# Neighbour sum: preparation two slots earlier, and values transposed by VectorE from 32x32 blocks instead of by TensorE

## The reference, cut to what matters

```python
            att = jax.nn.softmax(h[..., 0], axis=-1)
            xk = x.transpose(0, 2, 1)[bidx, idx]
            agg = jnp.einsum('bnkc,bnk->bnc', xk, att)
            return x + agg.transpose(0, 2, 1)
...
    x = _L2_xattn_ref(ctx_4096, x, L2_xattn_W1, L2_xattn_g1, L2_xattn_b1, L2_xattn_W2, L2_xattn_g2, L2_xattn_b2, L2_xattn_W3, L2_xattn_g3, L2_xattn_b3, 30)
    x = _L3_xattn_ref(x, ctx_4096, ctx_4096, ctx_4096, mask_Bx1x4096_ff1, L3_xattn_W_in, L3_xattn_b_in, L3_xattn_W_out, L3_xattn_b_out)
```

## Time and profile before

| | us |
|---|---|
| median of 3 runs | 6278.45 |
| lowest and highest | 6277.33 and 6285.72 |
| the profiled execution | 6277.67 |
| its span, first to last instruction | 6275.9 |
| TensorE matmuls busy in the span | 5497.9 (88%) |
| VectorE busy | 5659.0 (90%) |
| ScalarE busy | 4493.5 (72%) |
| GpSimd busy | 3395.9 (54%) |

### The profile page before, as it was taken

How to read it: one execution, slowest core, us unless ns; L and a number is a source line. 1 busy time by engine, 2 the same in 40 slices (tenths; PEclk the granted TensorE clock), 3 DMA queues, 4 the chain that set the end, 5 groups by cost and what they waited for, 6 DMA issues and landing times. The chain is left out here.

```text
span 6275.9 us, 227278 instructions
## 1 busy us (share of the span) xinstructions
PE 5497.9 (88%) x82516; PEld 3378.3 (54%) x82516; DVE 5659.0 (90%) x8045; ACT 4493.5 (72%) x17145; POOL 3395.9 (54%) x3471
## 2 busy tenths in 40 slices
PE   7888989889888888888898888898669769999999
PEld 3555555555555555555555555555423347777776
DVE  7999999999999999999999999999755787777776
ACT  7888888888888888888888888888605623333333
POOL 3466666666666666666666666666720033333332
PEclk9999999999999999999999999999789879999999
DMA  2333333333333333333333333333340023333332
GB/s 45 95 105 99 99 99 97 92 99 108 99 111 92 100 98 97 98 106 102 106 98 99 99 98 98 99 108 96 105 99 0 0 70 94 88 85 88 89 93 71
DMA packets 651349, 568.72 MB, mean 91 GB/s; under 512 B 553072, under 2 KB 574832, under 8 KB 616208
## 3 DMA queue, kind: packets, MB, share of 16 engines
q1 hardware_dynamic: 613264, 284.51, 19.3%
q10 hardware_dynamic: 36864, 268.45, 12.2%
HBM read 384.76 MB, written 67.24 MB: 72 GB/s over the span
## 5 line engine op out<-in xcount | busy, mean ns | idle before, releaser
L725 ACT ACTIVATE prob<-SC,row_max 128x64 f32<-128x64 f32 x6144 | 1835.6, 335 | 336.1 <-DVE row_max L1059 327.2
L838 POOL TENSOR_TENSOR prob<-prob,row_rec 128x512 f32<-128x512 f32 x768 | 800.6, 1042 | 1394.3 <-DVE row_rec L1067 1389.4
L725 ACT ACTIVATION_READ_ACCUMULATOR prob<-SC,row_max 128x1 f32 x6144 | 1387.8, 228 | 0.0
L1051 DVE FIND_INDEX8 nbr<-top,dist 128x8 uint16<-128x1024 f32 x1024 | 1234.3, 1217 | 0.0
L1044 DVE MAX8 top<-dist 128x8 f32<-128x1024 f32 x1024 | 1190.6, 1203 | 1.7 <-DVE dist L1046 0.2
L1046 DVE MATCH_REPLACE8 dist<-top,dist 128x1024 f32<-128x1024 f32 x768 | 923.4, 1207 | 0.0
L589 PE MATMUL SC<-k_bd,q_t 128*64 128x256 f32 x6144 | 902.7, 418 | 0.0
L1710 ACT ACTIVATE dense<-DM 128x512 f32<-128x512 f32 x512 | 305.4, 596 | 749.9 <-PE DM L1669 749.4
L1818 DVE TENSOR_TENSOR d_oh_a<-lo,iota_a 128x4096 bf16<-128x4096 bf16 x256 | 583.7, 2290 | 242.2 <-PE DM L1669 241.7
L610 PEld LDWEIGHTS PT<-ident,prob 128*128 128x128 f32 x3072 | 364.0, 144 | 812.3 <-issue 789.1
L610 PE MATMUL PT<-ident,prob 128*128 128x128 f32 x3072 | 487.8, 283 | 334.2 <-ACT prob_t L732 333.5
(11 more groups left out here) (189 smaller groups left out, 9437.9 us busy)
## 6 DMA issues: line engine op xcount, KB each, us to landing
low_all<-low_scratch ACTq DMA_DIRECT2D x256, 1024.0 KB, 5.0
k_bd<-k_t SPq DMA_DIRECT2D x3072, 16.0 KB, 1.9
placed<-compact SPq DMA_DIRECT2D x256, 192.0 KB, 3.8
ctx<-in_ctx SPq DMA_DIRECT2D x32, 512.0 KB, 5.9
mask<-in_mask SPq DMA_DIRECT2D x32, 512.0 KB, 8.5
xb<-in_x SPq DMA_DIRECT2D x32, 512.0 KB, 3.3
x_scratch<-xb SPq DMA_DIRECT2D x32, 512.0 KB, 6.8
y_scratch<-y_b SPq DMA_DIRECT2D x32, 512.0 KB, 6.4
```

What stands on the lines that cost most here:

```text
L725: last = act.activation(prob[:, s % 4, g * CHUNK:(g + 1) * CHUNK], SC[:, s % 2, g * CHUNK:(g + 1) * CHUNK], ACT.Exp, bias=row_max[:, s % 2 ...
L838: pool.tensor_tensor(pr, pr, row_rec[:, r % 2, :].unsqueeze(2).to_broadcast([128, 8, CHUNK]), ALU.mult).then_inc(normed, 1)
L1051: last = dve.max_index(nbr[:, uu % BPB, t, k * 8:(k + 1) * 8], best, row)
```

## The change

TensorE's transposes, `XT`, the identity and ScalarE's copy of `XT` are gone. The values are loaded a second time: ScalarE's queue issues four DMAs per batch (`by_quarters`), each of which fills 32 partitions of `x2_q` with pieces of 32 values (128 bytes), 1024 pieces a DMA, laid out so that a transpose inside each 32x32 block gives the whole transpose. VectorE does that transpose in one instruction of 128x1024 (`turn_quarters`) straight into `x2_t`, one batch ahead. x2 is still loaded as before, for GpSimd's addition. Besides, VectorE's steps stand in other slots: `indices` in 0, `weights` in 1, `one_hot_blocks` in 2, the moments in 3, `compact_blocks` in 4 and 5, and the new transpose in 6. ScalarE copies the weights after bank 0 instead of bank 1 and issues the four DMAs after bank 2.

```diff
@@ sync, body
-                        sp.wait_ge(xt_ready, START + before(1, 1))
-                        sp.sem_inc(passed, 1)
@@ tensor, weighted_sum and body
-                    pe.wait_ge(xt_copied, START + b(1, 1))
+                    pe.wait_ge(xt_ready, START + b(1, 1))
...
-                pe.wait_ge(x2_in[u], START + (i + 1) * 16)
-                pe.wait_ge(xt_copied, START + b(1))
-                for t in range(NT):
-                    last = pe.transpose(XT[:, t // 4, (t % 4) * 128:(t % 4 + 1) * 128], x2[:, u, t * 128:(t + 1) * 128], ident[:, :])
-                last.then_inc(xt_ready, 1)
@@ scalar
+            def by_quarters(batch):
+                rows = dram["x2"][batch].rearrange("(w c) (t q m) -> q c t w m", w=4, q=4, m=32)
+                for q in range(4):
+                    dst = x2_q[32 * q:32 * q + 32, :].rearrange("c (t w m) -> c t w m", w=4, m=32)
+                    act.dma_start(dst, rows[q]).then_inc(quarters_in, 16)
...
-                act.wait_ge(xt_ready, START + b(1, 1))
-                if not is_first(i, u):
-                    act.wait_ge(summed, START + b(2, -1))
-                act.activation(x2_t[:, u, :, :].rearrange("p t c -> p (t c)"), flat(XT[:, :, :]), ACT.Identity).then_inc(xt_copied, 1)
...
-                    if x == 1 and not is_last(i, u):
+                    if x == 0 and not is_last(i, u):
                         weights(counter(i, u + 1))
+                    if x == 2 and not is_last(i, u):
+                        act.wait_ge(xt_ready, START + b(1, 1))
+                        by_quarters(b(1, 1))
...
+            by_quarters(0)
             weights(counter(0, 0))
@@ vector
+            def turn_quarters(b, u, read_before):
+                dve.wait_ge(quarters_in, START + b(64, 64))
+                if read_before is not None:
+                    dve.wait_ge(summed, START + read_before)
+                dve.sem_inc(passed, 1)
+                dve.transpose(x2_t[:, u, :, :].rearrange("p t c -> p (t c)"), x2_q[:, :]).then_inc(xt_ready, 1)
...
+                    if t in (4, 5) and not is_last(i, u):
+                        compact_blocks(counter(i, u + 1), i, (u + 1) % BPD, t - 4)
+                    if t == 6 and not is_last(i, u):
+                        turn_quarters(counter(i, u + 1), (u + 1) % BPD, None if is_first(i, u) else b(2))
...
             indices(counter(0, 0), 0, 0)
+            turn_quarters(counter(0, 0), 0, None)
             weights(counter(0, 0))
```

More of the change, by code:

```diff
@@ L1493, in sem @@
             return counts[-1]
-        ident = sb("d_ident", [128, 128])
         iota = sb("iota_a", [128, 128], BF16)
@@ L1514, in neighbour_sum @@
         y3 = sb("d_y3", [128, BPD, T])
+        x2_q = sb("x2_q", [128, T])
         x2_t = sb("x2_t", [128, BPD, NT, 128])
@@ L1522, in neighbour_sum @@
         DM = ps("DM", [128, DM_BANKS, 512])
-        XT = ps("XT", [128, 2, 512])
         AG = ps("AG", [128, 2, 512])
@@ L1540, in neighbour_sum @@
         dense_copied = sem("dense_copied")
+        quarters_in = sem("quarters_in")
         xt_ready = sem("xt_ready")
-        xt_copied = sem("xt_copied")
         summed = sem("summed")
@@ L1553, in neighbour_sum @@
         passed = sem("d_passed")
-        CONSTS = [(ident[:, :], "ident"), (iota[:, :], "iota_a"), (iota_m[:, :], "iota_m"), (minus_half[:, :], "pow_half")]
+        CONSTS = [(iota[:, :], "iota_a"), (iota_m[:, :], "iota_m"), (minus_half[:, :], "pow_half")]
         block = es.enter_context(nc.Block())
@@ L1868, in body @@
                     spread(b, i, u, t)
+                    if t == 0 and not is_last(i, u):
+                        indices(counter(i, u + 1), (u + 1) % BPD, i + (u + 1) // BPD)
+                    if t == 1 and not is_last(i, u):
+                        weights(counter(i, u + 1))
                     if t == 1 and not is_first(i, u):
@@ L1871, in body @@
                     if t == 2 and not is_last(i, u):
[L1872 to L1875, removed]
+                        one_hot_blocks(counter(i, u + 1))
+                    if t == 3 and not is_first(i, u):
                         moments_of(counter(i, u - 1), (u - 1) % BPD)
[L1877 to L1880, removed]
+                    if t in (4, 5) and not is_last(i, u):
+                        compact_blocks(counter(i, u + 1), i, (u + 1) % BPD, t - 4)
+                    if t == 6 and not is_last(i, u):
+                        turn_quarters(counter(i, u + 1), (u + 1) % BPD, None if is_first(i, u) else b(2))
             dve.memset(placed[:, 0, :, :, :, :], 0.0).then_inc(cleared[0], 1)
             indices(counter(0, 0), 0, 0)
+            turn_quarters(counter(0, 0), 0, None)
             weights(counter(0, 0))
```

## The result

The changed kernel took 6296.8 us (median; 6292.85 to 6303.59), 1.003 times the kernel before, 95% interval 1.0021 to 1.0039. The forecast was 6253, range 6238 to 6268, so it was wrong in size and in sign: 19 us slower (against 6277.6 for the kernel before, run beside it) where 25 faster was forecast. The profiled execution took 6292.85 us, its span is 6291.0.

The account below looks back on a forecast made before the run. TensorE was taken to carry the neighbour sum (busy 472 of 500 us), VectorE near (391). The terms 33.9 - 3.4 - 1.6 - 3.1 - 0.8 = 25.0 us came off 6278.45, giving 6253 us, range 6238 to 6268.

Parts of the forecast that it names:

- Step 1: TensorE's batch edges: without XT, 21.6 us gained at 17 plain edges, 12.3 at 14 jump edges (0.87 each); gap stays.
- Steps 2 to 4: VectorE's waits: next d_oh_a 0.2 us at 17 edges, moved moments 0.05 at 31, new transpose (1.20 us) 0.1 at 31.
- rival (slot 7): VectorE becomes the bound at slot 7: transpose 1.75 us, hold 2.8, spread 7 late by 0.45; 6266 us, chance 0.17.
- Steps 5 and 6: ScalarE's four DMA issues, 2.3 us (7.5 worst), and the quarters' landing, 3.5 to 10 us: both hidden, no cost.
- Step 8: Start of the neighbour sum: one constants DMA fewer, but the new transpose on the path to the first DM; cost 0.8 us.
- The rivals: Full gain 6238 us (0.13); slot 7 6266 (0.17); second GpSimd hold 6295 (0.06); late quarters, over 6600 or 6281 (0.04).
- the loop gap grows: Sign that the forecast is wrong: TensorE's idle at the loop's jump, expected to keep its 3 to 4 us, gets longer.

Follow-up runs that it names:

- a_pad34: Changed kernel with 68 waits on a long-past event (34 instructions that do nothing) ahead of TensorE's loop; 6252.3 us, ratio 0.9959 to the kernel before.
- a_pad290: Changed kernel with 580 waits on a long-past event (290 instructions) ahead of TensorE's loop; 6251.0 us, ratio 0.9958 to the kernel before.
- a_pad33: Changed kernel with 66 waits on a long-past event (33 instructions) ahead of TensorE's loop; 6250.5 us, ratio 0.9956 to the kernel before.
- a_pad98: Changed kernel with 196 waits on a long-past event (98 instructions) ahead of TensorE's loop; 6306.7 us, ratio 1.0049 to the kernel before.

## Why the prediction was wrong, point by point

- **What bounds the kernel**: right. TensorE carried it, and every us of the result stands in TensorE's order.
- **Step 1**: the step that failed, in the sentence "The gap itself stays, since the jump stays". It put a change of the idle time at a jump at nothing. The first gap does stay, 3.70 and 3.74 us, but a second one of 3.35 to 3.66 us came at each of 13 jumps: that it is one gap depended on where TensorE's code lies, and taking instructions out ahead of the loop moved it. The price, against a_pad34, is 3.66 us a turn "to AG" and 0.40 of AG at the low clock. The gain itself was there: at equal place (a_pad34 against before) a jump edge loses 1.79 us "to AG", of which 0.29 come back in AG and 0.21 in the gap (whose mean lies between 3.7 and 4.0 in all kernels but two, so this part may be chance), so 1.29 net where 0.87 was forecast.
- **Steps 2 to 4** (waits of 0.2, 0.05 and 0.1 us an edge): the rest of the turn, which holds the edge without a jump, is 0.97 us shorter at equal place. The forecast has 1.27 - 0.2 for this edge, less 0.15 for each of two batches: 0.77. The waits were a little too dear. The transpose is 1.23 us for 1.20 forecast, at no time 1.75 or 2.5; its rival (slot 7) did not come about.
- **Steps 5 and 6**: nothing, as forecast, though the issues take 4.04 us in the batch shown, nearer to the 2.3 than to the worst 7.5. The quarters land in 3.5 us at the median, under the 10 us allowed. Both were hidden.
- **Step 8**: it can't be read to a microsecond, since the first DM starts between 5074 and 5084 us in the executions of kernels that are alike up to there.
- **The sum**: 25.0 us off 6278.45, and a_pad34, a_pad290 and a_pad33 give 29, 26 and 26 us less than the kernel before beside them. So the terms were near for the kernel that I thought I was forecasting, but that the sum meets 6253 so well is partly luck: 13 turns are 29 us shorter in a_pad34 than before, where the terms gave 21 (13 x 1.64), and in its profiled execution the first DM begins 5.9 us later, which no term had.
- **The rivals**: all four were about waits between engines. What came true, more idle time at the jump, was nearest to "the loop gap grows", which stood only in the last sentence on what would make the forecast wrong and had no chance and no price. The trace of before held the hint: the longest idle of TensorE was laid to nothing, and I took its length as fixed without asking what sets it.

## What to carry to other kernels

Where the trace shows an engine idle at a loop's jump and lays it to nothing, it may be the time to fetch code, as it was here, and its length is then a property of the program's layout: an edit that changes the count of an engine's instructions ahead of the loop can double it. Look when the packets of the instruction queue land: here an engine short of code went on 1.2 to 1.9 us behind one. Their count alone can miss it, as a_pad98 shows. Repeat a surprising result with some instructions of padding before believing a theory about the edit. Better still, write the loop out for the one engine whose loop is longer than a piece: here that was worth 110 us against the changed kernel and 66 against a_pad34, more than twice the change itself.

## What was not expected of the hardware

- TensorE fetches code in pieces of 256 instructions (16 KB); a jump back into a loop of 3264 costs 3.7 to 4.0 us of idle time on the mean when a full piece lies behind the target (3.2 to 4.3 each) and 7.5 to 8.5 with one instruction of it. The second piece can run some 4 us after the first has begun to run, however little the first holds.
- A second short stall soon after the first is dearer than its length: the granted clock is still 0.50 where it was 0.82 without the stall, and the distance from the AG block to DM 1 is 5.4 and 5.8 us on the mean where it was 4.3 (3.52 at the full clock).
- VectorE, ScalarE, GpSimd and SyncE with 57 to 104 instructions a turn jump back in under 0.1 us: 6186.2 us with their loops and 6186.6 without.
- Code that runs straight on can outrun its fetch too: with no jump at all TensorE still stalls 12 times in 900 us, 6.8 us in all. The ten stalls of 0.25 us or more stand behind 184 to 261 small matmuls in a row and end 1.3 to 1.5 us after an instruction packet landed.
- One VectorE transpose of 128x1024 float32 in 32x32 blocks takes 1.23 us, and a DMA of 1024 pieces of 128 bytes is issued in 0.59 us at the median and lands in 3.5.
